# Attention scores on Trainium2: heads in pairs as two row tiles of TensorE, in two fp32r parts instead of three of bf16

## What is computed

```python
x = layernorm(x)
q, k, v = x @ W_Q.T, x @ W_K.T, x @ W_V.T      # each into 16 heads of 16
scores = q @ k.T / sqrt(16)
scores = where(causal_mask, scores, -inf)
p = softmax(scores, axis=-1)
o = p @ v
```

## Time and profile before

| what | value |
|---|---|
| median of 3 runs | 2883.01 us (2882.04 to 2885.75) |
| the profiled execution | 2887.01 us |
| its span, first to last instruction | 2885.3 us |
| mean granted clock of PE | 0.942 |
| PE busy over the span | 2644.5 us, 92% |
| DVE, ACT, POOL busy | 1707.9, 1413.5, 792.8 us |

### The profile page before, as it was taken

How to read it: one execution, slowest core, us unless ns; L and a number is a source line. 1 busy time by engine, 2 the same in 40 slices (tenths; PEclk the granted TensorE clock), 3 DMA queues, 4 the chain that set the end, 5 groups by cost and what they waited for, 6 DMA issues and landing times. The chain is left out here.

```text
span 2885.3 us, 50333 instructions
## 1 busy us (share of the span) xinstructions
PE 2644.5 (92%) x17194; PEld 2126.3 (74%) x17194; DVE 1707.9 (59%) x3298; ACT 1413.5 (49%) x2605; POOL 792.8 (27%) x803
## 2 busy tenths in 40 slices
PE   7899999979979999699999999999999999995574
PEld 6444444458758888589898998999999998984452
DVE  6688888626678888654555445454554545548321
ACT  6377777756558877633333333333333333337310
POOL 3521212100052222132222222222222222223574
PEclk9799999989989999799999999999999999986665
DMA  8964646030055544322222222222222222224476
GB/s 250 211 107 65 87 64 88 4 100 3 4 213 185 189 187 176 110 59 52 60 52 57 52 62 49 50 59 52 60 52 59 53 50 60 51 57 156 109 172 124
DMA packets 413585, 263.19 MB, mean 91 GB/s; under 512 B 257952, under 2 KB 375616, under 8 KB 404608
## 3 DMA queue, kind: packets, MB, share of 16 engines
q1 hardware_dynamic: 405104, 245.69, 33.6%
q0 software_dynamic: 8256, 14.52, 2.9%
HBM read 183.93 MB, written 80.40 MB: 92 GB/s over the span
## 5 line engine op out<-in xcount | busy, mean ns | idle before, releaser
L1888 POOL TENSOR_TENSOR lin_o2sum<-lin_o2sum,lin_o 128x512 f32<-128x512 f32 x128 | 185.4, 1448 | 930.6 <-ACT lin_o L1931 930.6
L875 DVE TENSOR_REDUCE score_pm<-score_SM 128x1 f32<-128x512 f32 (+3 forms) x608 | 364.2, 655 | 80.4 <-PE score_SM L735 47.6
L829 ACT ACTIVATE score_PR<-score_SE 128x512 f32<-128x512 f32 (+1 forms) x640 | 309.7, 558 | 106.1 <-PE score_SE L763 102.5
L2121 DVE TENSOR_TENSOR C_acc<-lin_OUT,C_acc 128x512 f32<-128x512 f32 x256 | 176.2, 691 | 244.5 <-PE lin_OUT L2022 242.9
L1978 PE MATMUL lin_PJ<-C_XH,lin_WH 128*128 128x512 f32 x774 | 254.3, 410 | 8.4 <-DVE lin_WL L2101 8.4
L1908 ACT ACTIVATE lin_qT<-lin_PJ 128x512 f32<-128x512 f32 x129 | 77.0, 597 | 377.6 <-PE lin_PJ L1978 370.5
L735 PE MATMUL score_SM<-A_KR,A_QR 96*128 96x512 bf16 (+3 forms) x768 | 228.8, 339 | 13.5 <-DVEq L81 10.1
L1978 PE MATMUL lin_PJ<-C_XL,lin_WH 128*128 128x512 f32 x774 | 241.0, 392 | 0.0
L1978 PE MATMUL lin_PJ<-C_XH,lin_WL 128*128 128x512 f32 x774 | 240.2, 392 | 0.0
L763 PE MATMUL score_SE<-A_QR,A_KR 99*128 99x512 bf16 (+3 forms) x768 | 210.5, 330 | 2.0 <-ACT score_PR L829 1.5
L1936 ACT ACTIVATE lin_goh<-lin_go 128x512 fp32r<-128x512 f32 x128 | 81.0, 633 | 250.9 <-DVE lin_go L2165 250.9
(11 more groups left out here) (354 smaller groups left out, 6515.0 us busy)
## 6 DMA issues: line engine op xcount, KB each, us to landing
experts_sq<-B_roots SPq DMA_DIRECT2D x64, 1024.0 KB, 4.7
k_turned<-lin_kblk SPq DMA_DIRECT2D x113, 256.0 KB, 2.0
lin_krow<-k_turned SPq DMA_DIRECT2D x452, 64.0 KB, 2.4
A_QR<-q_parts SPq DMA_DIRECT2D x96, 128.0 KB, 6.5
A_KR<-k_parts SPq DMA_DIRECT2D x96, 128.0 KB, 6.8
kept_GU<-L_ffn_gate_up_proj SPq DMA_DIRECT2D x48, 192.0 KB, 3.0
v_rows<-inp_vt SPq DMA_DIRECT2D x32, 256.0 KB, 4.1
A_V<-v_rows SPq DMA_DIRECT2D x16, 512.0 KB, 10.8
```

Source lines behind the costliest of these rows:

```text
L829: nc.scalar.activation(PR[:, st % BUFS, h, 0:width], SE[:, e % RING, 0:width], ACT.Exp, scale=SCALE)\
L875: nc.vector.tensor_reduce(pm[:, n % 2, h0:h0 + nh, t, k0 // CHUNK], SM[:, count % RING, 0:nh * nk].rearrange("p (h k) -> p h k", h=nh), AX ...
L1888: nc.gpsimd.tensor_tensor(o2sum[:, c], o2sum[:, c], o2[:], ALU.add).then_inc(pool_sum, 1)
L2121: nc.vector.tensor_tensor(dst, OUT[:, half], dst, ALU.add).then_inc(dve_acc[half], 1)
```

## The change

What it does, part by part:

- **Two parts of fp32r** instead of three of bf16, and three products instead of six: a head takes 3 x 16 = 48 rows and two rows for the maximum, 50 in place of 99.
- **Pairs of heads.** An even head lies in rows 0 to 63, an odd one in rows 64 to 127 (LANE = 64). A matmul then has a tile of 64 rows, and the two of a pair are issued one behind the other, into two banks. Masks and transposes stay tiles of 128 rows, V stays four column tiles.
- **Maxima** in 20 pieces of two banks (both heads of a pair, up to 1024 elements per reduce), in a ring of two such pairs of banks. One mask matmul per bank. The output transposes take a place in this ring, the bank TR goes.
- **Scores** in pairs over the same three single banks; a pair takes two of them. The transposed maxima are one transpose of 128 x 64 instead of eight, and take one place in that ring.
- **A new ORDER** in pairs (S4.1 is the second pair of step 4), with SHIFT = 12.
- **Input phase.** The middle parts on ACT and DVE and the third on POOL go; the second part is DVE's one subtraction. Stores are 2 x 128 x 512 of fp32. The ones in KR are written here by POOL.
- **Loads.** NLOAD stays 13 for a unit (12 of 16 rows by two heads, one of values). The maxima come back by four DMAs instead of one.

```diff
-TERMS = 3
-QK_TERMS = ((0, 0), (0, 1), (1, 0), (1, 1), (0, 2), (2, 0))
+PAIRS = HG // 2
+TERMS = 2
+QK_TERMS = ((0, 0), (0, 1), (1, 0))
+LANE = P // 2
-NLOAD = 2 * len(QK_TERMS) + 1
+NLOAD = 2 * 2 * len(QK_TERMS) + 1
...
-            for n in range(CHUNKS * R):
-                r = n % R
...
-                nc.gpsimd.tensor_tensor(parts[:, r, 2], rest[:, r], parts[:, r, 1], ALU.subtract).then_inc(low, 1)
+            for c in range(2):
+                nc.gpsimd.memset(KR[c * LANE + 32:(c + 1) * LANE].bitcast(F32), 1.0).then_inc(lane_rows, 1)
...
-                nc.vector.tensor_tensor(rest[:, r], PQ[:, r], parts[:, r, 0], ALU.subtract).then_inc(rest_ready, 1)
-                if r % 2 == 0:
-                    nc.vector.tensor_tensor(parts[:, r, 1], PQ[:, r], parts[:, r, 0], ALU.subtract).then_inc(mid_dve, 1)
+                nc.vector.tensor_tensor(parts[:, r, 1], PQ[:, r], parts[:, r, 0].bitcast(F32), ALU.subtract)\
+                    .then_inc(low, 1)
...
-    SHIFT = 20
+    SHIFT = 12
-    ORDER = ("S1.0 S1.1 M M S1.2 S1.3 S2.0 M M S2.1 V0 S2.2 M S2.3 S3.0 M S3.1 S3.2 M M S3.3 M S4.0 M "
...
+    ORDER = ("S1.0 M S1.1 V0 S2.0 M S2.1 M S3.0 M M S3.1 V1 S4.0 M V2 M S4.1 M S5.0 M S5.1 V3 S6.0 M M S6.1 V4 "
+             "R M S7.0 M V5 S7.1 M S8.0 M V6 S8.1 M V7 S9.0 M M S9.1 V8 S10.0 O0 M V9 S10.1 M O1")
...
-        SM = ph.ps("SM", [P, RING, CHUNK])
+        SM = ph.ps("SM", [P, BANKS, 2, CHUNK])
...
+                for j in range(np):
+                    for c in range(2):
+                        rows = slice(c * LANE, c * LANE + ROWS_QK)
+                        ins = nc.tensor.matmul(SM[:, k % BANKS, c, j * nk:(j + 1) * nk], QR[rows, u, p0 + j, queries],
+                                               KR[rows, u, p0 + j, k0:k0 + nk], start=(j == 0), stop=not edge,
...
-                for t in range(QT):
-                    ins = nc.tensor.transpose(TRB[0:TERMS * HG, t * P:(t + 1) * P],
-                                              mparts[:, t].rearrange("p a h -> p (a h)"), identb[:])
+                nc.tensor.transpose(SE[0:QT * TERMS * HG, k % RING, 0:P],
+                                    mparts[:].bitcast(F32).rearrange("p t a h -> p (t a h)"), ident[:]).then_inc(m_tr, 1)
...
+                banks = [exp_free(("S", e + c)) % RING for c in range(2)]
...
+                    for c, bank in enumerate(banks):
+                        rows = slice(c * LANE, c * LANE + ROWS_ALL)
+                        ins = nc.tensor.matmul(SE[:, bank, at:at + nq], KR[rows, u, r, kt * P:(kt + 1) * P],
+                                               QR[rows, u, r, q:q + nq], start=True, stop=True)
```

More of the change, by code:

```diff
@@ L269, in attention_inputs_phase @@
         XL = ph.sb("XL", [P, 2, KD, CHUNK], F32R)
-        parts = ph.sb("parts", [P, R, TERMS, CHUNK], BF16)
-        rest = ph.sb("rest", [P, R, CHUNK])
+        parts = ph.sb("parts", [P, R, TERMS, CHUNK], F32R)
         vt = ph.sb("vt", [P, TPC, AH, VW])
@@ L588, in score_phase @@
         TURN.append((kind, part))
+    max_uses = [("M", c) for c in range(NP + SHIFT)]
+    exp_uses = [("R", 0)] + [("S", 2 * p + c) for p in range(PAIRS) for c in range(2)]
+    for n in range(UNITS):
+        for kind, part in TURN:
+            if kind == "M" and (n + 1) * NP + SHIFT + part[0] < UNITS * NP:
+                max_uses.append(("M", (n + 1) * NP + SHIFT + part[0]))
+            elif kind == "O":
+                max_uses.append(("O", 2 * n + part[0]))
+            elif kind == "S" and n * NSTEPS + part[0] < UNITS * NSTEPS:
+                exp_uses += [("S", n * NS + part[0] * HG + 2 * part[1] + c) for c in range(2)]
+            elif kind == "R" and n + 1 < UNITS:
+                exp_uses.append(("R", n + 1))
+    max_slot = {use: k for k, use in enumerate(max_uses)}
+    exp_slot = {use: k for k, use in enumerate(exp_uses)}
     with Phase(nc, "score") as ph:
@@ L710, in _ @@
                         max_parts(n + 1)
-                    if kind == "S" and part[1] == HG - 1 and CUTS[part[0] % NSTEPS]:
+                    if kind == "S" and part[1] == PAIRS - 1 and CUTS[part[0] % NSTEPS]:
                         if part[0] < NSTEPS:
@@ new lines, in max_piece, with max_free @@
+                if edge:
+                    future = mask_q[:].rearrange("p (o k) -> p o k", o=1).to_broadcast([P, np, P])
+                    for c in range(2):
+                        into = SM[:, k % BANKS, c, 0:np * nk].rearrange("p (j k) -> p j k", j=np)
+                        ins = nc.tensor.matmul(into[:, :, nk - P:nk], identb[:], future, start=False, stop=True,
+                                               skip_group_check=True)
+                ins.then_inc(pe_m, 1)
+            def max_free(use):
+                k = max_slot[use]
+                if k >= BANKS:
+                    kind, before = max_uses[k - BANKS]
+                    pe.wait_ge(dve_o if kind == "O" else dve_m, done(before))
+                return k
@@ L760, in scores @@
+            def scores(n, s, r):
+                half, g = STEPS[s]
+                u, e = n % SLOTS, n * NS + s * HG + 2 * r
+                if s == 0 and r == 0:
+                    pe.wait_ge(m_in[u], (n // SLOTS + 1) * 32 * PAIRS)
+                banks = [exp_free(("S", e + c)) % RING for c in range(2)]
                 items, _ = layout(half, GROUPS[half][g])
@@ L799, in _ @@
                     max_rows_out(0)
-            for h in range(HG):
-                scores(0, 0, h)
+            for r in range(PAIRS):
+                scores(0, 0, r)
             for n in range(UNITS):
@@ L848, in _ @@
             max_row(0)
-            for h in range(HG):
-                exps(0, 0, h)
+            for r in range(PAIRS):
+                exps(0, 0, r)
             for n in range(UNITS):
```

147 lines of the change are left out of this document (64 added, 83 removed), and 3 rows, old and new, of the table ORDER.

## The result

| | before | the change |
|---|---|---|
| median | 2884.38 us (4 runs, 2882.04 to 2887.95) | 2960.78 us (4 runs, 2934.38 to 2977.22) |
| ratio to before | | 1.0258, 95% interval 1.0218 to 1.0299 |
| profiled execution | 2887.01 us, span 2885.3 | 2971.65 us, span 2969.9 |
| mean granted clock of its span | 0.942 | 0.918 |

The change makes the kernel 2.6% slower, 76 us; forecast were 9 us. The four runs of the change lie 43 us apart, where those of before lie 6 apart, and they stand in the order of their mean granted clocks: 2934.38 at 0.932, 2949.92 at 0.927, 2971.65 at 0.918, 2977.22 at 0.916.

What follows compares the result with a forecast made beforehand. PE was taken to bound the score phase at full clock: 29.0 us a unit against 28.86, +7 for that phase, and +2 for input stores gave +9, 2892 us on the median; range 2838 to 2955.

Steps and rivals of the forecast that it cites:

- The pairs: Score phase: two 64-row tiles run together at the cost of one fp32r matmul, 8.7 us a unit instead of 15.9.
- not quite one matmul: Rival, score phase: a pair costs 1.3 matmuls, period 31 us, +30 against the forecast, 2922 us; chance .10.
- loads in series: Rival, score phase: a row tile's load waits for the matmul on the same rows, period 33, +60, 2952 us; chance .07.
- doesn't do what it says: Rival, score phase: a pair's tiles run one after the other, period 35.6, +100, 2992 us; chance .06.
- a change of shape: Score phase on PE: each change of tile shape costs .09 us, .12 out of V; 46 per unit, 4.5 us.
- an exposed load: Score phase on PE: each of 22 entries into row tiles pays .10 us for fp32r weights not loaded ahead.
- weights loaded ahead: Rival, score phase: row-tile weights load while masks or values run, period 27.2, −27, 2865 us; chance .22.
- masks change nothing: Rival, score phase: row and full tiles alternate without drain, period about 25.7, −48, 2844 us; chance .17.
- PE sets the pace ... at full clock: Score phase: PE is the bound, busy 50.00 of 50 us at full clock before the change.
- POOL's ones "0": Input phase: POOL's 14.20 us of ones move there under cover of its idle time, costing 0.
- The stores: Input phase: 32 stores of parts grow from 384 to 512 KB, taken as +2 us, bounds −2 and +9.
- a hand-over: Score phase: the hand-over back from ACT's exp to PE, estimated .05 us, in the loop of 1.1 us between pairs.

Runs made afterwards that it cites:

- e2: The change with one 128-row matmul in place of each pair of row tiles from the second unit on: 2889.46 us, ratio 1.0025.
- e1: The kernel before with two single banks instead of three for the scores, so PE waits for exps: 2957.84 us, ratio 1.0259.
- e5: e3 with POOL's ones in short writes and the odd head of each pair left out on PE from the second unit on: 3143.93 us, ratio 1.0896.
- e6: e3 with POOL's ones in short writes and one 128-row matmul in place of each pair from the second unit on: 2911.88 us, ratio 1.0092.
- e3: The change with each mask as two 64-row matmuls in the lane of its head: 2925.76 us, ratio 1.0156.
- f2: e3 with POOL's ones in short writes, another order of the same words and SHIFT 16: 2897.67 us, ratio 1.004.
- f3: f2 with SHIFT 8 and the order found best for it: 2884.71 us, ratio 0.9999.
- f4: f3 plus two unused full-row matmuls at each word M without a piece left, in units 14 and 15: 2876.66 us, ratio 0.9977.

## Why the prediction was wrong

**What held.** The pairs: full concurrency, and weight loads of both tiles hidden behind the pair before (.12 for 256 columns), so the rivals "not quite one matmul", "loads in series" and "doesn't do what it says" fall. The rule of the Trainium skill (page "TensorE: Matmul & The Clock Gate", section "Part 3: Packing small matmuls") that a load overlaps only matmuls of other rows, which spoke for the series case, disagrees with these rows too. The prices of a change of shape, .09, and of an exposed load, .10, came out on PE in the size carried over; so "weights loaded ahead" and "masks change nothing" fall as they were put. The reason for the load's price was wrong in part: behind masks it is paid without a change of shape too (e2, .31 for .23). ACT did stay where it was, and PE does wait for it ahead of scores (in the view of waits, 12 times in the three units at full clock). The period at full clock, the sum of all that, is 29.70 where 29.0 were worked out.

**The step that failed: "PE sets the pace ... at full clock".** Every price of the sum was taken at 2.4 GHz, because the windows of before show 1.00 once the prologue is over. The change replaces 96 and 99 rows by pairs of 48 and 50, and the clock does not stay. In the profiled execution the clock is 0.91 over 200 to 560 us. Of the 84.6 us lost, 43 stand in periods with half clock in them, over the 29.7 of those without, and the 24 at both ends of the phase lie largely at half clock too. No rival named it. A hint was there: the prediction counted rows only as room for two heads, and the clock of 0.71 in the prologue showed that this program does meet the lower level. What e1, e2, e5 and e6 show in its place, from 200 to 560 us: as many waits in full tiles leave the clock at 1.00 (e1), and so do nearly as many changes of shape (e6); with tiles of few rows it falls, to 0.91 in pairs and to 0.54 one at a time (e5). e3, f2 and f3 show that with such tiles in pairs fewer changes of shape and waits lower it less (0.97, 0.99, and 1.00 up to 540 us). The profile's busy share doesn't tell the cases apart. The Trainium skill, page "TensorE: Matmul & The Clock Gate", section "Part 1: The HAM clock gate", says that the clock goes by how busy PE has been; by the busy share of the profile the two stretches at full clock disagree, for e5 is the busier one (5.96 of 6.60 us against 5.46 in e2) and its clock falls.

**The second step: POOL's ones "0".** The cover that was named, POOL's idle time in the input phase, was there, but the price was not POOL's time: it is DVE's, which waits for the whole write. 7.6 us. The stores were +0.7 where +2 was taken.

**Terms that were mis-sized.** The period is .7 us over the one that was walked; a hand-over of .11 for .05, 14 times a unit, would make that up, but was not measured apart. And the path: the masks' changes of shape are worth .8 us on the period (e3, e6), not the 3.4 us of PE's work that e3's expectation put on them. Some of that was never gained (the exposed load stays), and for the rest waits for exps and reduces come up behind them. For the change itself this made little difference, for what it could gain much. The prologue, put at 0, took 29.1 us up to its transposed maxima where it took 25.7, at half clock throughout. The sum has a slip, too: 14 periods of .14 are 2 us, not 3; nothing hangs on it.

**The chances.** Slower had .43, and the mechanism that came is none of the cases that carried it, so the chance that the right direction had, it had for other reasons: luck. The range ended at 2955, 6 us under the median.

## What to carry to other kernels

Before a matmul is cut into tiles of fewer rows, ask what holds the clock up besides it: time won on the engine is given back if the granted clock falls, and the busy share won't show it; look at the clock of each stretch. Where a stretch is bound elsewhere, a few full-row matmuls into a bank that nobody reads can be worth their time (8 us here for 56 of them; whether by their rows or by the waits they fill was not tried apart). And a long write on GpSimd is not free where GpSimd is idle: cut it into short ones if VectorE has small passes on a path beside it.

## What the runs showed of the hardware that was not expected

- Two 64-row tiles of 48 or 50 rows run at the time of one, 3 ns apart, with fp32r operands, and loads of 202 ns hide behind the pair before (256 columns, .12). Yet over 200 to 560 us the granted clock is 0.54 with one such tile at a time (e5), 0.91 with two in this change, 1.00 with 128 rows (e2, e6).
- A weight load of .19 us behind two masks of 128 columns costs some .08 even where no shape changes (512 columns take .31 for .23 in e2, .32 between row tiles in e3).
- A 14 us stretch of GpSimd writes made a VectorE pass of 0.17 us last 2.92 and 4.56 us, to the end of the write under way.
- The change scatters from run to run with the granted clock (2934 to 2977 on the same data); e1 and e6, with full rows, do not (2955 to 2960, 2910 to 2914, two runs each), nor does f4 (2875.5 to 2880.4).
